# A graph layer on one core: one-hot columns by destination modulo 128, strip halves added on VectorE, means scaled on ScalarE, one-column counts, dense work in pieces

## The chip, the cores and the metric

The kernel runs on one core of one Trainium2 chip. The metric is the time of the whole program on the device in microseconds (us); lower is better. TensorE is called PE below, VectorE DVE, ScalarE ACT, GpSimd POOL and SyncE SP, as in the profile.

## The reference

For 12500 nodes with 256 features and 212500 edges (sorted by destination):

```
xn   = layernorm(x)
sum  = segment_sum(xn[src], dst);  cnt = segment_sum(1, dst)
agg  = sum / max(cnt, 1)
gnn  = relu(agg @ W_l.T + b_l + xn @ W_r.T) + xn
q, k, v = xn @ wq + bq, xn @ wk + bk, xn @ wv + bv        # 8 heads of 32
q, k = elu(q) + 1, elu(k) + 1
mix  = (q (k^T v)) / (q sum(k) + 1e-6) @ wo + bo
x1   = x + gnn + mix
out  = x1 + mixture_of_experts(layernorm(x1))             # the 2 best of 8 experts, then a layernorm
```

## The kernel before

Stage 1 normalises all rows and writes them to a table in HBM, each row as two float16 halves of 256 (a high and a low part, scaled by XS = 2048), and builds the matrices of the linear attention (`M_s`, `KS_s`). Stage 3, the subject here, goes over NB = 49 blocks of BN = 256 nodes. Stage 5 is the two-expert layer.

A block of stage 3 has TB = 34 edge tiles of 128 edges (the last block 29, so 1661 in all). For each tile POOL issues one indirect DMA (L643) that gathers 128 rows of the table, by the indices in `idxb`, into `msgs` (in the buffer `ring`). DVE makes the tile's one-hot matrix in float16 by comparing `iota_f` with the destinations in `edges` (`one_hots`, L1334; output `oh`, in the buffer `ohh`), and PE multiplies it with the gathered rows (L1076, into `pa`) and adds up the counts as a row (L1093, into `pc`: 128 columns, or two times 64).

Tiles come in 8 batches a block (`BATCH`). POOL waits for `idx_ready` and for `batch_used` of the same batch one block back; PE waits at each batch for `oh_ready` and for `gathered0` to `gathered7`; DVE waits in `one_hots` for `batch_used` half a block back. Each tile covers a window of 128 nodes that starts at `LO[k]`, a multiple of STRIP = 64. The sums of the tiles of one window are taken by DVE from PSUM (`take_strip`, L1354) as a strip, which overlaps its neighbours by half. When the block is over, PE joins its five strips by matmuls with an identity (`join_strips`, L1042), which also turns them, features to the partitions. The count row goes through ACT (`count_row`, L805) and a matmul with ones (`spread_counts`, L1003) to all partitions, where DVE makes a reciprocal of 256 (L1345) and scales the sums (`neighbours`, L1348).

The dense work of a block lies between its tiles, in each engine's own written order: `products` (L1015, 12 matmuls in float32), `turn_xn` (L981), `queries` (L990), `normalizers` (L997) and `turn_y` (L1027) on PE; `middle` (L1361 to L1369), `residual` (L1381, L1383), `middle_stats` (L1184 to L1214), `query_features` (L1388) and `normalise_queries` (L1394 to L1398) on DVE. The work of block b on block b - 1 starts at tile 6, `products` at tile 11, `normalizers` at tile 22.

## Time and profile before

| what | value |
|---|---|
| time, median of 3 runs (lowest, highest) | 3031.16 us (3028.17, 3031.72) |
| time of the profiled execution | 3025.19 us |
| its span, first to last instruction | 3023.7 us |
| first and last gather start | 264.2 us, 2376.4 us |
| PE, DVE, ACT, POOL busy over the span | 82%, 57%, 26%, 66% |

The table's shares are averages over three stages. Stage 3 is the stretch between the first and the last gather and a few microseconds after, some 70% of the span. POOL's busy time there is the gathers alone; the time between two of them is not counted as busy.

### The profile page before, as it was taken

What the parts mean: (1) busy time and instruction counts of PE and PEld (TensorE: products, weight loads), DVE (VectorE), ACT (ScalarE), POOL (GpSimd) and SP (SyncE); (2) the same over time, 40 slices, a digit from 0 to 9 for tenths busy, and PEclk for the clock granted to TensorE, in tenths of its full rate; (3) what the DMA queues carried; (4) which work ended last, traced back from release to release, by engine and by line L of the source; (5) the groups of instructions that cost most, each with busy time, mean ns of one, the idle gap of its engine ahead of it and who ended that gap; (6) DMA issues with size and microseconds to landing.
All of it is one profiled execution on the core that took longest, in us unless ns stands there. A gap on an engine that the chain in (4) does not pass through costs nothing.

```text
span 3023.7 us, 38535 instructions
## 1 busy us (share of the span) xinstructions
PE 2475.3 (82%) x11532; PEld 1605.7 (53%) x11532; DVE 1724.4 (57%) x3502; ACT 774.0 (26%) x1810; POOL 1991.1 (66%) x1831
## 2 busy tenths in 40 slices
PE   6888778787887788778877887788778699999997
PEld 5665434443444344434444444444444388888886
DVE  7885455445545554555455545554555566666666
ACT  4553011111111111111111111111111155555554
POOL 5446777777777777777777777777777334444443
PEclk9998777877787777777877787877777799999999
DMA  5333344434444444444444444444444322111221
GB/s 143 107 101 97 115 125 123 120 116 123 125 118 118 124 124 116 122 124 125 116 121 124 124 118 120 124 126 116 121 123 125 94 70 62 62 62 62 66 75 49
DMA packets 192238, 327.01 MB, mean 108 GB/s; under 512 B 32703, under 2 KB 138216, under 8 KB 192200
## 3 DMA queue, kind: packets, MB, share of 16 engines
q0 software_dynamic: 80160, 219.14, 25.4%
q1 hardware_dynamic: 111624, 107.01, 11.3%
q10 hardware_dynamic: 416, 0.39, 0.1%
q8 instruction: 19, 0.31, 0.0%
q14 instruction: 19, 0.16, 0.0%
HBM read 275.21 MB, written 51.20 MB: 108 GB/s over the span
## 4 chain that ended last, share of the span: by engine, by line
POOL 28%; PE 26%; issue 20%; DVE 15%; DMA 7%; ACT 2%; POOLq 0%; DVEq 0%; ACTq 0%; SPq 0%
POOL ring L643 20%; PE pd L1015 8%; PE pa L1076 6%; PE pd L1042 6%; DMA ring<-xn_table,idxb 4%; PE pc L1093 2%; POOL work L672 2%; POOL work L657 2%; POOL work L655 2%; DVE bst L1184 2%; PE pc L1003 2%; DMA work<-x_rows 2%; DVE nh L1211 1%; DMA out<-work 1%; DVE nv L1206 1%
## 5 line engine op out<-in xcount | busy, mean ns | idle before, releaser
L643 POOL DMA_INDIRECT ring<-xn_table,idxb x1661 | 1607.5, 968 | 509.7 <-issue 489.9
L1076 PE MATMUL pa<-ring,ohh 128*128 128x512 f16 x1661 | 767.7, 462 | 222.5 <-DMA ring<-xn_table,idxb 206.5
L1354 DVE TENSOR_REDUCE ring<-pa 128x256 f32<-128x512 f32 x196 | 135.4, 691 | 586.1 <-PE pa L1076 585.5
L1093 PEld LDWEIGHTS pc<-ohh,ones_h 128*1 128x1 f16 x2045 | 133.7, 80 | 535.7 <-issue 535.7
L1093 PE MATMUL pc<-ohh,ones_h 128*1 128x128 f16 (+1 forms) x2045 | 384.7, 219 | 0.0
L1076 PEld LDWEIGHTS pa<-ring,ohh 128*128 128x128 f16 x1661 | 173.1, 104 | 350.1 <-issue 172.1
L1136 PE MATMUL pd<-parts 128*128 128x256 f32 (+1 forms) x1568 | 314.6, 284 | 33.8 <-DVE parts L1524 33.8
L1136 PEld LDWEIGHTS pd<-parts 128*128 128x128 f32 (+1 forms) x1568 | 253.4, 188 | 51.4 <-DVE parts L1524 44.4
L1334 DVE TENSOR_TENSOR ohh<-iota_f,edges 128x512 f16<-128x512 f32 (+1 forms) x391 | 272.8, 718 | 0.9 <-issue 0.9
L997 PE MATMUL pd<-work,KS_s 128*128 128x256 f32 x196 | 100.7, 669 | 198.6 <-DVE work L1388 198.6
L769 ACT ACTIVATE work<-pd 128x512 f32<-128x512 f32 (+1 forms) x49 | 29.2, 596 | 881.5 <-PE pd L981 881.5
L1042 PEld LDWEIGHTS pd<-ident,ring 128*128 128x128 f32 x976 | 204.8, 321 | 31.6 <-issue 31.3
L1136 PE MATMUL pd<-W_lo_t,parts 128*128 128x256 f32 x784 | 220.1, 281 | 0.0
L1042 PE MATMUL pd<-ident,ring 128*128 128x128 f32 (+1 forms) x976 | 213.4, 413 | 0.0
L655 POOL TENSOR_TENSOR work<-work,ohh 128x1024 f32<-128x1024 f32 (+1 forms) x25 | 62.8, 2511 | 212.9 <-DMA work<-x_rows 163.5
L1015 PE MATMUL pd<-mats,work 128*128 128x256 f32 x784 | 193.1, 390 | 0.0
L1524 DVE TENSOR_TENSOR parts<-ring,parts 128x512 fp32r<-128x512 f32 (+1 forms) x100 | 121.9, 1219 | 109.6 <-ACT parts L855 109.6
L997 PEld LDWEIGHTS pd<-work,KS_s 128*128 128x128 f32 x196 | 57.1, 322 | 214.0 <-DVE work L1388 205.4
L1396 DVE RECIPROCAL work<-work 128x512 f32<-128x512 f32 x49 | 164.3, 3353 | 1.7
L1015 PEld LDWEIGHTS pd<-mats,work 128*128 128x128 f32 x784 | 147.0, 193 | 21.9
L1136 PEld LDWEIGHTS pd<-W_lo_t,parts 128*128 128x128 f32 x784 | 147.3, 188 | 7.9
L1524 DVE TENSOR_TENSOR parts<-M_s,parts 128x512 fp32r<-128x512 f32 (+1 forms) x100 | 100.1, 1001 | 71.7 <-ACT parts L855 71.5
(188 smaller groups left out, 3684.0 us busy)
## 6 DMA issues: line engine op xcount, KB each, us to landing
ring<-xn_table,idxb POOLq DMA_INDIRECT x1661, 2.7
yT<-in_x SPq DMA_DIRECT2D x24, 512.0 KB, 4.0
xn_table<-ring SPq DMA_DIRECT2D x24, 512.0 KB, 4.8
work<-in_x SPq DMA_DIRECT2D x48, 256.0 KB
x_rows<-work SPq DMA_DIRECT2D x48, 256.0 KB
y_rows<-work SPq DMA_DIRECT2D x48, 256.0 KB
work<-y_rows SPq DMA_DIRECT2D x24, 512.0 KB, 4.3
work<-x_rows SPq DMA_DIRECT2D x24, 512.0 KB, 4.0
```

Source lines behind the costliest of these rows:

```text
L643: pool.indirect_dma_start(out=msgs[:, k, :, :].rearrange("p s d -> p (s d)"), out_offset=None, in_=xn_table[:, :], in_offset=bass.Indirect ...
L655: pool.tensor_tensor(y_in[u][:, 0:n, :], y_in[u][:, 0:n, :], b2m[:, :].unsqueeze(1).to_broadcast([P, n, D]), ALU.add).then_inc(s["yb_made" ...
L997: ins = mm(pd[:, 0, c * BN:(c + 1) * BN], KS_s[:, c, :], pq[:, c * BN:(c + 1) * BN], start=True, stop=True)
L1015: ins = mm(pd[:, 2 + h, at:at + D], a[:, c * BN + h * P:c * BN + (h + 1) * P], w[:, c, :], start=a is xT2 and c == 0, stop=a is not xT2 an ...
L1042: ins = mm(pd[:, 0, c * BN + c0:c * BN + c1], strips[:, (NS * u + t + 1) % KEPT, c * P:(c + 1) * P], ident[:, c0 - STRIP * t:c1 - STRIP * ...
L1076: ins = mm(pa[:, t % 2, :], oh[:, slot, :], msgs[:, k, :, :].rearrange("p s d -> p (s d)"), start=begins, stop=ends, skip_group_check=True)
L1093: ins = mm(pc[0:1, v, c0:c1], ones_h[:, 0:1], oh[:, slot, o0:o1], start=first, stop=closing, skip_group_check=True)
L1136: ins = mm(pd[0:n, 2 * u + t // 2, (t % 2) * D:(t % 2 + 1) * D], hp[:, t * P:t * P + n], wp[:, f, :], start=f == 0 and t % 2 == 0 and hp i ...
L1334: V.tensor_tensor(oh[:, slot:slot + m, :], bc(iota_f[:, :], m), where, ALU.is_equal)\
L1354: V.tensor_reduce(strips[:, (NS * u + t + 1) % KEPT, :], pa[:, t % 2, :].rearrange("p (s d) -> p d s", s=PARTS), AX.X, ALU.add)\
L1396: V.reciprocal(qb, qb).then_inc(s["nrm_rec"], 1)
L1524: V.tensor_tensor(h_lo[f % HS][:, 0:w], h_full[f % 2][:, 0:w], h_hi[f % HS][:, 0:w], ALU.subtract)\
```

## The change

The window of a tile is no longer counted from `LO[k]`: the column of a destination is the destination modulo 128 (`iota_f` has 64 more columns, and `one_hots` reads it from `LO % 128`). So the two halves of a block's own strips sit on the partitions where the neighbouring strips have theirs. DVE adds the halves (`join_strips`, now on DVE: one instruction on 64 partitions for both groups, two on the other 64), each a sum of two operands in SBUF. The counts are a column beside each strip's sums: PE makes it with the one-hot as weights and one column of ones, DVE copies it from PSUM in `take_strip`, adds it with the halves and takes the reciprocal of 128x2. ACT scales the strips (`scale_sums`), PE turns them by 4 transposes (`turn_sums`), and DVE copies them from PSUM (`take_sums`). `count_row` and `spread_counts` are gone. PE's dense work is cut into pieces of one half each that go ahead of single tiles (`DENSE`), and batches now end where windows end.

```diff
-    BATCH = [(0, 4), (4, 8), (8, 12), (12, 17), (17, 21), (21, 25), (25, 29), (29, 34)]
+    BATCH = [(0, 4), (4, 8), (8, 13), (13, 17), (17, 21), (21, 25), (25, 30), (30, 34)]
...
-        strips = ring[:, MSGS:MSGS + KEPT * D].rearrange("p (n d) -> p n d", d=D)
+        strips = ring[:, MSGS:MSGS + KEPT * SW].rearrange("p (n d) -> p n d", d=SW)
...
+            def scale_sums(d, u):
+                act.wait_ge(s["cnt_rec"], d + 1)
+                for g in range(2):
+                    own = strips[:, NS * u + 2 * g + 1, 0:D]
+                    ins = nc.scalar.activation(own, own, ACT.Copy, scale=cnts[:, g:g + 1])
+                ins.then_inc(s["strips_scaled"], 1)
...
-            def count_row(d, v):
-                act.wait_ge(s["agg_done"], d + 1)
-                wait(act, s["agg_taken"], d)
-                nc.scalar.activation(rc[0:1, :], pc[0:1, v, 0:BN], ACT.Copy).then_inc(s["cnt_row"], 1)
...
+                    if not is_int(b, 0):
+                        scale_sums(b - 1, 1 - u)
...
+            def product(a, w, at, d, h):
                 for c in range(C):
+                    ins = mm(pd[:, 2 + h, at:at + D], a[:, c * BN + h * P:c * BN + (h + 1) * P], w[:, c, :],
+                             start=a is xT2 and c == 0, stop=a is not xT2 and c == C - 1, skip_group_check=True)
+                return ins
...
+            def neighbour_product(d, h):
+                pe.wait_ge(s["agg_taken"], d + 1)
+                ins = product(aggS, wlT, 0, d, h)
+                if h == 1:
+                    ins.then_inc(s["o_made"], 1)
...
-            def join_strips(d, u):
-                sums = strip_sums(d)
-                pe.wait_ge(s["strip_taken"], NS * d + len(sums))
+            def turn_sums(d, u):
+                pe.wait_ge(s["strips_scaled"], d + 1)
                 wait(pe, s["nrm_eps"], d + 1)
-                for t in sums:
-                    c0, c1 = max(STRIP * t, 0), min(STRIP * t + P, BN)
+                for g in range(2):
                     for c in range(C):
-                        ins = mm(pd[:, 0, c * BN + c0:c * BN + c1], strips[:, (NS * u + t + 1) % KEPT, c * P:(c + 1) * P],
-                                 ident[:, c0 - STRIP * t:c1 - STRIP * t], start=t == -1 and c == 0, stop=t == sums[-1],
-                                 skip_group_check=True)
+                        ins = nc.tensor.transpose(pd[:, 0, c * BN + g * P:c * BN + (g + 1) * P],
+                                                  strips[:, NS * u + 2 * g + 1, c * P:(c + 1) * P], ident[:, :])
                 ins.then_inc(s["agg_made"], 1)
-            JOIN = 6
-            HOOKS = ((11, products, 1), (11, turn_xn, 0), (13, queries, 0), (22, normalizers, 0), (26, turn_y, 1))
+            DENSE = {1: (root_product, 0, 1), 2: (root_product, 1, 1), 3: (mixed_product, 0, 1),
+                     4: (mixed_product, 1, 1), 12: (neighbour_product, 0, 1), 13: (neighbour_product, 1, 1),
+                     16: (queries, 0, 0), 17: (queries, 1, 0), 24: (normalizers, 0, 0), 25: (normalizers, 1, 0)}
+            TURN_SUMS, TURN_X, TURN_Y = 9, 14, 27
...
-                        if k == JOIN and not is_int(b, 0):
-                            spread_counts(b - 1, 1 - u)
-                            join_strips(b - 1, 1 - u)
-                        for at_tile, work, back in HOOKS:
-                            if k == at_tile and not (back and is_int(b, 0)):
-                                work(b - back)
+                        dense(b, k, u)
...
-                        ins = mm(pa[:, t % 2, :], oh[:, slot, :], msgs[:, k, :, :].rearrange("p s d -> p (s d)"),
-                                 start=begins, stop=ends, skip_group_check=True)
-                        if ends:
-                            ins.then_inc(s["strip_done"], 1)
-                        parts = []
-                        for db in (-1, 0, 1):
-                            c0, c1 = max(LO[k], db * BN), min(LO[k] + WIN, (db + 1) * BN)
-                            if c0 < c1 and not (db < 0 and is_int(b, 0)) and not (db > 0 and last_block):
-                                parts.append((db, c0 - db * BN, c1 - db * BN, c0 - LO[k]))
-                        for db, c0, c1, o0 in parts:
-                            v = (u + db) % 2
-                            first = (db == 1 and LO[k - 1] + WIN <= BN) or (is_int(b, 0) and k == 0)
-                            if db == 1 and first:
-                                wait(pe, s["agg_taken"], b)
-                            closing = (db == -1 and LO[k + 1] >= 0) or (last_block and k == LAST - 1)
-                            o1 = o0 + c1 - c0
-                            ins = mm(pc[0:1, v, c0:c1], ones_h[:, 0:1], oh[:, slot, o0:o1], start=first, stop=closing,
-                                     skip_group_check=True)
-                            if closing:
-                                ins.then_inc(s["agg_done"], 1)
-                    if ks and not (last_block and ks[-1] == LAST - 1):
+                        mm(pa[:, t % 2, :], oh[:, slot, :], msgs[:, k, :, :].rearrange("p s d -> p (s d)"),
+                           start=begins, stop=ends, skip_group_check=True)
+                        ins = mm(pc[:, t % 2, 0:1], oh[:, slot, :], ones_h[:, 0:1], start=begins, stop=ends,
+                                 skip_group_check=True)
+                    if ks:
                         ins.then_inc(s["batch_used"], 1)
...
-                V.tensor_tensor(oh[:, slot:slot + m, :], bc(iota_f[:, :], m), where, ALU.is_equal)\
+                c0 = LO[ks[0]] % WIN
+                V.tensor_tensor(oh[:, slot:slot + m, :], bc(iota_f[:, c0:c0 + WIN], m), where, ALU.is_equal)\
                     .then_inc(s["oh_ready"], 1)
-            def neighbours(d, u):
-                dve.wait_ge(s["cnt_spread"], d + 1)
+            def join_strips(d, u):
+                low, high = slice(0, STRIP), slice(STRIP, P)
+                own = strips[:, NS * u + 1:NS * u + 4:2, :]
+                last = is_int(d, NB - 1)
+                dve.wait_ge(s["strip_taken"], NS * d + (NS if last else NS + 1))
+                V.tensor_tensor(own[low, :, 0:D + 1], own[low, :, 0:D + 1], strips[low, NS * u:NS * u + 3:2, 0:D + 1], ALU.add)\
+                    .then_inc(s["halves_added"], 1)
+                for g in range(1 if last else 2):
+                    V.tensor_tensor(own[high, g, 0:D + 1], own[high, g, 0:D + 1],
+                                    strips[high, (NS * u + 2 * g + 2) % KEPT, 0:D + 1], ALU.add)\
+                        .then_inc(s["halves_added"], 1)
+                dve.wait_ge(s["halves_added"], 3 * d + (2 if last else 3))
+                V.tensor_scalar(cnts[:, :], own[:, :, D], 1.0, XS, ALU.max, ALU.mult).then_inc(s["cnt_max"], 1)
+                dve.wait_ge(s["cnt_max"], d + 1)
+                V.reciprocal(cnts[:, :], cnts[:, :]).then_inc(s["cnt_rec"], 1)
+                dve.wait_ge(s["cnt_rec"], d + 1)
+            def take_sums(d):
                 wait(dve, s["o_made"], d)
                 wait(dve, s["x1_made"], d)
-                wait(dve, s["agg_taken"], d)
-                V.tensor_scalar(rc[:, :], pc[:, u, BN:2 * BN], 1.0, XS, ALU.max, ALU.mult).then_inc(s["cnt_max"], 1)
-                dve.wait_ge(s["cnt_max"], d + 1)
-                V.reciprocal(rc[:, :], rc[:, :]).then_inc(s["cnt_rec"], 1)
-                dve.wait_ge(s["cnt_rec"], d + 1)
                 dve.wait_ge(s["agg_made"], d + 1)
-                V.tensor_tensor(pair(aggS), pair(pd[:, 0, :]), bc(rc[:, :], 2), ALU.mult)\
-                    .then_inc(s["agg_taken"], 1)
+                V.tensor_copy(aggS, pd[:, 0, :]).then_inc(s["agg_taken"], 1)
             def take_strip(b, t, u):
-                dve.wait_ge(s["strip_done"], NS * b + t + 2)
-                V.tensor_reduce(strips[:, (NS * u + t + 1) % KEPT, :], pa[:, t % 2, :].rearrange("p (s d) -> p d s", s=PARTS),
-                                AX.X, ALU.add)\
-                    .then_inc(s["strip_taken"], 1)
+                dve.wait_ge(s["batch_used"], NBT * b + 2 * t + 3)
+                kept = strips[:, (NS * u + t + 1) % KEPT, :]
+                V.tensor_reduce(kept[:, 0:D], pa[:, t % 2, :].rearrange("p (s d) -> p d s", s=PARTS), AX.X, ALU.add)
+                V.tensor_copy(kept[:, D:D + 1], pc[:, t % 2, 0:1]).then_inc(s["strip_taken"], 1)
...
-                    neighbours(d, 1 - u)
+                    join_strips(d, 1 - u)
+                    take_sums(d)
                     middle(d)
                     middle_stats(d)
                     return
                 for q in range(3):
                     one_hots(b, q)
                 take_strip(b, -1, u)
+                if not is_int(b, 0):
+                    join_strips(d, 1 - u)
                 one_hots(b, 3)
                 if not is_int(b, 0):
-                    neighbours(d, 1 - u)
+                    take_sums(d)
```

On DVE, at the start of the work of block b on block b - 1: before, after the strip of the tiles that end the old block (`ring<-pa`, with `ring` holding the strips). `rc` holds the counts and `work` the block's operands.

```order
L1354 TENSOR_REDUCE ring<-pa 128x256 [waits strip_done]
L1334 TENSOR_TENSOR ohh<-iota_f,edges 128x640 [waits batch_used]
L1343 TENSOR_SCALAR rc<-pc 128x256 [waits x1_made,agg_taken,o_made,cnt_spread]
L1345 RECIPROCAL rc<-rc 128x256 [waits cnt_max]
L1348 TENSOR_TENSOR work<-pd,rc 128x512 [waits agg_made,cnt_rec]
L1334 TENSOR_TENSOR ohh<-iota_f,edges 128x512 [waits batch_used]
```

The same place in the changed kernel, with its own line numbers:

```order
L1366 TENSOR_REDUCE ring<-pa 128x256 [waits batch_used]
L1367 COPY ring<-pc 128x1
L1343 TENSOR_TENSOR ring<-ring 64x2x257 [waits strip_taken]
L1346 TENSOR_TENSOR ring<-ring 64x257 x2
L1350 TENSOR_SCALAR cnts<-ring 128x2 [waits halves_added]
L1352 RECIPROCAL cnts<-cnts 128x2 [waits cnt_max]
L1334 TENSOR_TENSOR ohh<-iota_f,edges 128x512 [waits batch_used,cnt_rec]
L1360 COPY work<-pd 128x512 [waits agg_made,x1_made,o_made]
```

Three additions with both inputs in `ring` have come in, and the reciprocal is over 2 columns in place of 256; the 512-element operation on `pd` is a copy.

On PE, before, from the second batch of a block on (`gathered1`): the join stands in one piece between the tiles.

```order
L1076 MATMUL pa<-ring,ohh 128x512 [waits strip_taken,gathered1,oh_ready]
L1093 MATMUL pc<-ohh,ones_h 1x128
L1076 MATMUL pa<-ring,ohh 128x512
L1093 MATMUL pc<-ohh,ones_h 1x128
L1003 MATMUL pc<-rc,ones 128x256 [waits cnt_row]
L1042 MATMUL pd<-ident,ring 128x64 [waits nrm_eps,strip_taken]
L1042 MATMUL pd<-ident,ring 128x64
L1042 MATMUL pd<-ident,ring 128x128 x6
L1042 MATMUL pd<-ident,ring 128x64 x2
```

The changed kernel, from its third batch on:

```order
L1091 MATMUL pa<-ring,ohh 128x512 [waits gathered2,oh_ready]
L1093 MATMUL pc<-ones_h,ohh 128x1
L1045 MATMUL pd<-ident,ring 128x128 [waits nrm_eps,strips_scaled]
L1045 MATMUL pd<-ident,ring 128x128 x3
L1091 MATMUL pa<-ring,ohh 128x512
L1093 MATMUL pc<-ones_h,ohh 128x1
L1091 MATMUL pa<-ring,ohh 128x512
L1093 MATMUL pc<-ones_h,ohh 128x1
L1091 MATMUL pa<-ring,ohh 128x512
L1093 MATMUL pc<-ones_h,ohh 128x1
L1009 MATMUL pd<-mats,work 128x256 [waits agg_taken]
L1009 MATMUL pd<-mats,work 128x256
```

Ten matmuls and the spreading of the counts have become four transposes that stand three tiles later, and the product with the neighbours' means follows in two pieces at tiles 12 and 13 instead of behind the other products at tile 11.

## Rows read from the trace of the kernel before

**Rows 1.** The page: span, busy line, granted clock in 40 slices.

```profile
span 3023.7 us, 38535 instructions
...
PE 2475.3 (82%) x11532; PEld 1605.7 (53%) x11532; DVE 1724.4 (57%) x3502; ACT 774.0 (26%) x1810; POOL 1991.1 (66%) x1831
...
PEclk9998777877787777777877787877777799999999
```

**Rows 2.** Line L643 (the gathers): ns min/median/max, starts, idle before them.

```profile
L643 POOL DMA_INDIRECT ring<-xn_table,idxb x1661: 942/946/1599, 264.2 to 2376.4; - x185
...
  issue: 489.9, 1596
  ACT idxb L732: 10.1, 33
  PE pc L1093: 9.8, 32
...
DMA to landing us min/median/max: 2.6/2.7/4.3
```

**Rows 3.** Timeline, three stretches: start us, us, engine, line, [idle before].

```profile
382.38 1.27 POOL L643 DMA_INDIRECT ring<-xn_table,idxb  x1 [0.30 <-issue]
...
728.67 0.95 POOL L643 DMA_INDIRECT ring<-xn_table,idxb  x1 [0.30 <-issue]
729.13 0.69 DVE L1381 TENSOR_TENSOR work<-work 128x512 f32<-128x512 f32 x1
729.85 0.69 DVE L1383 TENSOR_TENSOR work<-work,bo_b 128x512 f32<-128x512 f32 x1
729.92 1.44 POOL L643 DMA_INDIRECT ring<-xn_table,idxb  x1 [0.30 <-issue]
...
2372.43 1.17 POOL L643 DMA_INDIRECT ring<-xn_table,idxb  x1 [0.30 <-issue]
```

**Rows 4.** Timeline, around DVE's reciprocal of 512.

```profile
1431.45 3.35 DVE L1396 RECIPROCAL work<-work 128x512 f32<-128x512 f32 x1
...
1432.18 0.95 POOL L643 DMA_INDIRECT ring<-xn_table,idxb  x1 [0.30 <-issue]
```

**Rows 5.** Groups in 1200 to 1800 us: count, busy us, mean ns, idle before.

```profile
L1334 DVE TENSOR_TENSOR ohh<-iota_f,edges 128x512 f16<-128x512 f32 x84 | 55.2, 685 | 0.0
...
L790 ACT ACTIVATE work<-work,nmr,rstd 128x256 f32<-128x256 f32 x28 | 15.3, 592 | 71.4 <-DVE nmr L1214 71.4
...
L1210 DVE TENSOR_TENSOR nh<-ny 128x2 f32<-128x2 f32 x42 | 6.8, 162 | 1.5
```

**Rows 6.** Groups in 268 to 280 us, on DVE.

```profile
L1316 DVE COPY yT<-pd 128x512 f32<-128x512 f32 x1 | 0.7, 693 | 0.4 <-PE pd L957 0.4
...
L1319 DVE TENSOR_TENSOR yT<-pd,yT 128x256 f32<-128x256 f32 x1 | 0.4, 424 | 2.9 <-PE pd L964 2.9
```

**Rows 7.** Groups in 1200 to 1800 us (14 blocks), on PE.

```profile
L1076 PE MATMUL pa<-ring,ohh 128*128 128x512 f16 x475 | 218.7, 460 | 60.3 <-DMA ring<-xn_table,idxb 60.1 <-issue 0.2
L1093 PE MATMUL pc<-ohh,ones_h 128*1 128x128 f16 (+1 forms) x586 | 109.7, 219 | 0.0
...
L1042 PE MATMUL pd<-ident,ring 128*128 128x128 f32 (+1 forms) x280 | 62.0, 417 | 0.0
```

**Rows 8.** Windows: busy of PE, PEld, DVE, ACT, POOL, clock, DMA share, GB/s.

```profile
1400.00:1800.00 400.00, 321.18 (x1311) 176.87 (x1311) 205.93 (x375) 56.74 (x201) 304.12 (x315) 0.77 0.42 121
1405.00:1408.00 3.00, 3.00 (x16) 3.00 (x16) 1.82 (x2) 0.00 (x0) 2.39 (x3) 0.50 0.41 126
```

**Rows 9.** The chain that ended last, 2384 to 2394 us: start us, us, what.

```profile
2384.98 0.38 ACT rc L805
...
2386.10 1.98 PE pd L1042 x16
2388.08 5.20 PE pd L1015 x24
2393.30 0.70 DVE work L1361
```

81 lines of the change are left out of this document (44 added, 37 removed).

## The prediction

> **What bounds the kernel now.** I read the page first, for which engine is full [rows 1]: PE looks fullest, 82% of the span, but its granted clock swings between the two levels in the middle stage, and POOL, at 66%, has nothing in the other stages that would show it as the bound. So I went to the gathers by themselves [rows 2]. From the first start at 264.2 us to the last at 2376.4 us lie 2112.2 us and 1660 steps, 1.272 us each. The median gather takes 0.946 us. The idle time before all 1661 is 489.9 + 10.1 + 9.8 = 509.8 us, 0.307 us each; the single rows show 0.30 [rows 3], also where a semaphore is named as the releaser. That gap is POOL's own step from one gather to the next, not a wait: no buffer, no index and no PE work has held a gather back. 0.946 + 0.303 is 1.249 us, and 1660 of those are 2073 us. What is left, about 39 us, is gathers that took longer than the median: mean 968 ns (1607.5 us of busy time over 1661) less 946 ns, times 1661, is 36.5 us, and a few us more lie in front of the first ones. Stage 3 is therefore 2073 us of gathers back to back, plus 36 us of stretched gathers, plus a tail behind the last gather.
>
> What stretches a gather is seen in the timeline [rows 3]. The gather at 728.67 runs its 0.95 us. The next starts at 729.92, 0.07 us after DVE began L1383, an addition with both inputs in SBUF; it takes 1.44 us, 0.49 longer, and the addition ends at 730.54, 0.62 us into the gather. DVE's long reciprocal with a single input runs over a whole gather and leaves it at 0.95 us [rows 4]. I set all 1661 gather rows beside DVE's rows. 129 gathers took over 1.0 us, and in 128 of them a DVE instruction with two SBUF inputs was running 0.1 us after the gather's start; the gather then lasts until that instruction ends and some 0.82 us more. An instruction that begins later, or has ended by then, costs nothing. Summed by DVE line: one_hots (L1334, 391 instructions) 24.3 us over 83 gathers; L1383 (49) 6.2 us over 14, the first and last of them at 382.38 and 2372.43 [rows 3]; L1381 (49) 4.1 us over 19; L1364 (49) 0.8; L1388 (49) 0.3; L1398 (49) nothing. So it is the phase of an instruction against the gathers that decides, and lines differ from 0 to 0.13 us per instruction.
>
> **The change part by part.** PE: the join's 280 matmuls in 14 blocks took 62.0 us [rows 7], 4.4 us a block; four transposes at its mean of 0.22 us are 0.9, so 3.5 us less. The count matmuls took 109.7 us in 14 blocks, 7.8 a block; 34 one-column ones cost at least nothing and at most the 0.10 us that I allow for a second pass of the weights, some 3.4, so at least 4.4 us less. The spreading of the counts goes too. PE gets about 8 us of 43.3 us a block back (34 x 1.272). None of it reaches the end: PE waits 60.3 us for gathers in those 14 blocks already [rows 7], and gathers do not wait for PE. It grows PE's waits for landings, no more. Nor does a gather start to wait for `idxb`: ACT issues the indices of the next block's first batches ahead of its new scaling, and the others are wanted a third of a block or more later.
>
> DVE: out go the reciprocal over 256, the scaling from PSUM and a short operation on PSUM, all with at most one SBUF input; by rows 4 they held up no gather, so removing them gives nothing. In come per block a copy from PSUM of 512 (0.69, [rows 6], one input: nothing), 4 copies of one column (0.16, after the smallest instruction [rows 5]: nothing, from PSUM), two tiny steps, and the join: one addition of 64 x 2 x 257 elements, in length like 128x512 (0.69, as one_hots, [rows 5]), and two of 64x257 (0.42 each, as 128x256, [rows 6]). All three have both inputs in SBUF. No row shows them. From below: nothing, as L1398 in all its 49. From above: every block stretches one gather by the longest seen, 1.599 - 0.946 = 0.65 us, and a second by a short one, 0.3: 0.95 x 48 = 46 us. I take the rate of the two additions in the middle of a block that are triggered as this one is, by work of PE whose clock varies: (4.1 + 6.2) / 98 = 0.105 us per 0.69 us instruction. What an instruction costs goes with the square of its length (the chance to be hit, times what remains), so a 0.42 us one costs 0.37 of that: 0.105 x 1.74 = 0.18 us a block, **+9 us** over 48 blocks.
>
> The Trainium skill, page "SBUF — State Buffer", section "Who interferes with whom", has two things on this. An instruction of DVE with two SBUF inputs contends with a GpSimd instruction that reads SBUF, and the loser waits for the whole instruction; with evenly spread phases that makes (0.69^2 + 2 x 0.42^2) / 2 / 1.25 = 0.33 us a block, 16 us, nearly twice what I take. The same section infers that tensor_tensor does not hold up descriptor generation; by that the join costs nothing. The stretched gathers [rows 3] are on the side of the first; the second is a rival below.
>
> The tail: after the last tile ACT's count row starts at 2384.98 and `middle` at 2393.30 [rows 9], 8.3 us. Now: strip 0.69 and column 0.16, additions 0.69 + 0.42, two tiny steps 0.4, scaling 2 x 0.59 [rows 5], four transposes 0.9, copy 0.69, and the last third of the products 5.20 / 3 = 1.7 [rows 9]: 6.8, and some 0.5 for the handovers, 7.3: 1 us less. The last tile itself can end earlier. Its gather starts at 2376.4 and lands 2.7 us later [rows 2], so four tiles at 0.7 us (L1076 0.46 and L1093 0.22, [rows 7]) could be done by 2382; now it is 2385, since PE is behind. With join and spreading off PE this comes 1 to 3 us sooner, less if `normalise_queries` (0.69 + 3.35 + 0.69) is then what DVE still has in front of the last strip. Together **-3.5 us** (-1 to -5).
>
> Stages 1 and 5 are not touched. The existing stretches, 36 us, are drawn anew: each batch now ends, and each one-hot starts, at another phase. I put no shift on them in the sum and +-15 us in the range.
>
> Sum against the profiled execution: 3025.2 + 9 - 3.5 = 3030.7 us. That execution is 6.0 us under the median of the runs, so from the median: 3031.2 + 5.5 = **3036.5 us**. A measurement of this kernel can tell about 0.2%, 6 us, from no change.
>
> **The rivals.**
> A. The forecast: the gathers stay the bound, the join costs about 9 us, old stretches stay within 7 us. 3036.5, own range 3029 to 3044. Chance 0.38.
> B. The one-hots fall into a bad phase. PE now often starts a batch right at its landing, so each `batch_used` and the one-hots behind it recur at one phase in every block. For: many of the 391 one-hots do sit in tight phases today, and cost 0.06 us each, half of L1381 and L1383's 0.105. If they go to that, 391 x 0.043 = +17 us on top: 3031.2 + 5.5 + 17 = 3054. Against: the phase could as well be good. It decides from where a one-hot still runs 0.1 us into a gather. Chance 0.24, clearly slower.
> C. The phases turn out better: one-hots and middle fall by half, -18 us, join +5: 3031 - 3.5 + 5 - 18 = 3015. For: L1398 and L1388 show lines with next to none. Chance 0.24, faster.
> D. The new additions cost nothing, the rest stays: 3031.2 - 3.5 = 3027.7, no change. Against: the stretched gathers [rows 3]. Chance 0.10.
> E. PE becomes the bound. Its granted clock is 0.50 (1.2 GHz) in one stretch, and 0.77 on the mean of 400 us, a mixture with the full 2.4 GHz [rows 8], where it is busy 0.80 x 43.3 = 34.7 us a block. Less 8 is 26.7, and all at 0.5 that is 26.7 x 0.77 / 0.5 = 41 us, plus the stalls behind DVE's query features. That touches 43.3; 1 us over it in 48 blocks is 3079. It decides when the clock never rises and DVE's results come late. For: more idle PE brings more low clock. Against: POOL has a block of slack. Chance 0.04. The Trainium skill, page "TensorE: Matmul & The Clock Gate", section "HAM oscillation", says that matmul bursts with waits between them fall back to the half clock each time; by that PE would sit low most of a block, which rows 8 show for part of it.
>
> **The numbers.** C ends below 3015 in some cases, B and E above 3054: range 3010 to 3060. Slower by over 0.2% (above 3037.2): B, E and two fifths of A, which straddles that bound, 0.24 + 0.04 + 0.15 = 0.43. Within: the rest of A and D, 0.23 + 0.10 = 0.33. Faster: C, 0.24.
>
> **What would show it.** Right: gathers still 0.30 us apart without a wait; busy time of the gather line near 1616 us (1607.5 + 9), the new stretches with the 64-partition additions running at their start; PE's waits for gathers above 60.3 us per 14 blocks; `middle` of the last block starting 12 to 16 us after the last gather's start in place of 16.9. Wrong: gaps above 0.30 before gathers (E, or indices late), a busy time of the gather line outside 1595 to 1630 (B, C), or the additions running over a gather's start without stretching it (D).

## The result, and the profile after

The changed kernel takes 3046.94 us (median of 6, 3041.0 to 3051.26), the kernel before in the same comparison 3029.54 us: a ratio of 1.0056, interval 1.0040 to 1.0072. It is slower by 17 us. Times and ratios here are of executions in the chip's faster state; one execution, of the additions alone below, fell in the slower one (3168.65 us, clock 0.683) and is left out. The profiled execution has a span of 3042.1 us, against 3023.7 before [rows 1].

The page of the kernel after, its span, busy line and granted clock:

```profile
span 3042.1 us, 36310 instructions
...
PE 2121.0 (70%) x10270; PEld 1450.6 (48%) x10270; DVE 1726.7 (57%) x3845; ACT 800.2 (26%) x1859; POOL 2009.3 (66%) x1831
...
PEclk9998767776776677767767777777667699999999
...
POOL 52%; issue 25%; DVE 9%; DMA 6%; PE 5%; ACT 2%; POOLq 1%; DVEq 0%; ACTq 0%; SPq 0%
```

PE went from 82% to 70% of the span, and the kernel became slower all the same: the engine that the change relieves is not the one that sets the end. The last line is the chain that ended last: POOL and its issue steps are 77% of it.

Groups by line of the kernel after (count, busy us, mean ns, idle before and its releasers), answering to [rows 2, 5, 6, 7], and the window that answers to [rows 8]:

```profile
L645 POOL DMA_INDIRECT ring<-xn_table,idxb x1661 | 1625.0, 978 | 509.8 <-issue 498.0 <-ACT idxb L734 10.4 <-PE pc L1093 1.5
L1091 PE MATMUL pa<-ring,ohh 128*128 128x512 f16 x1661 | 710.6, 496 | 780.2 <-DMA ring<-xn_table,idxb 645.0 <-DVE ohh L1334 122.5 <-issue 11.7
L1093 PE MATMUL pc<-ones_h,ohh 128*128 128x1 f16 x1661 | 314.7, 189 | 0.0
L1366 DVE TENSOR_REDUCE ring<-pa 128x256 f32<-128x512 f32 x196 | 135.4, 691 | 658.5 <-PE pc L1093 658.0
```
```profile
1400.00:1800.00 400.00, 251.14 (x1053) 143.72 (x1054) 202.46 (x434) 61.26 (x207) 305.23 (x312) 0.70 0.42 120
```

Idle time before the gathers is 509.8 us, as before; no gather waits for more than its 0.30. Their busy time grew by 17.5 us (1607.5 to 1625.0), and the last gather starts 17.5 us later (2393.9 against 2376.4). PE's busy time in the window fell from 321.18 to 251.14 us, 7.6 us a block of 43.3, and all of that went into waits: for landings it waits 645.0 us now, 206.5 before. A new wait for the one-hots, 122.5 us against 3.9, lies there too. The granted clock fell from 0.77 to 0.70, without touching the end. So this is a loss on POOL, whose code the change leaves alone.

Where it sits, from the timeline of the kernel after. First `normalise_queries` of one block (reciprocal L1407, product L1409), then the join of a later one:

```profile
1219.94 3.35 DVE L1407 RECIPROCAL work<-work 128x512 f32<-128x512 f32 x1
...
1222.57 0.94 POOL L645 DMA_INDIRECT ring<-xn_table,idxb  x1 [0.30 <-issue]
1223.33 0.69 DVE L1409 TENSOR_TENSOR work<-work 128x512 f32<-128x512 f32 x1
1223.82 1.01 POOL L645 DMA_INDIRECT ring<-xn_table,idxb  x1 [0.30 <-issue]
...
1411.95 0.69 DVE L1366 TENSOR_REDUCE ring<-pa 128x256 f32<-128x512 f32 x1 [11.08 <-PE pc L1093]
1411.99 0.95 POOL L645 DMA_INDIRECT ring<-xn_table,idxb  x1 [0.30 <-issue]
...
1412.74 0.69 DVE L1343 TENSOR_TENSOR ring<-ring 64x514 f32<-64x514 f32 x1
1413.24 1.00 POOL L645 DMA_INDIRECT ring<-xn_table,idxb  x1 [0.31 <-issue]
1413.45 0.76 DVE L1346 TENSOR_TENSOR ring<-ring 64x257 f32<-64x257 f32 x2
...
1414.55 0.94 POOL L645 DMA_INDIRECT ring<-xn_table,idxb  x1 [0.30 <-issue]
```

The reciprocal, one input, is running when the gather at 1222.57 starts, and this gather keeps 0.94. L1409, two inputs in SBUF, still has 0.20 us to run when the gather at 1223.82 starts: 1.01. In the join the gather at 1411.99 runs beside the one-input L1366 and keeps 0.95; the one at 1413.24 starts inside L1343, two inputs in SBUF, which ends 0.19 us later: 1.00. The two L1346 start 0.21 us into this gather or later, end before the next, and cost nothing here. These two are small hits; the mean one at L1409 is 11.7 / 38 = 0.31 us.

I set all gather rows beside DVE's rows once more. For each gather of more than 1.00 us I took what it has over 0.95 us, and summed by the DVE line that runs 0.1 us after its start (by this measure the kernel before has 35.4 us over 129 gathers):

| line of DVE | before | after |
|---|---|---|
| one-hots, L1334 | 24.0 us, 83 gathers | 20.6 us, 92 |
| product with the reciprocal, L1398 / L1409 | 0 | 11.7, 38 |
| query features, L1388 / L1399 | 0.3, 1 | 5.9, 31 |
| bias added to the rest, L1383 / L1394 | 6.2, 14 | 6.0, 16 |
| sum of the rest, L1381 / L1392 | 4.0, 19 | 1.6, 7 |
| join, L1343 and L1346 | none | 3.1 + 2.6, 10 and 16 |
| all (with small ones) | 35.4, 129 | 52.3, 218 |

The join, 5.7 us, is a third of the 16.9 us. The rest comes from two old instructions whose length didn't change, only the time of their start: together they gained 17.3 us, and other lines lost some 6.

The end, from the chain that ended last in the kernel after (start us, us, what), answering to [rows 9]:

```profile
2393.93 3.55 DMA ring<-xn_table,idxb
2397.48 0.14 issue
2397.61 0.59 PE pa L1091
...
2400.05 0.45 PE pa L1091
2400.49 0.00 PE pc L1093
2400.50 4.92 PE pd L1009 x16
2405.42 0.45 PE pd L1045 x4
...
2405.99 0.70 DVE work L1360
2406.69 0.04 issue
2406.74 2.01 PE pd L1009 x8
2408.74 0.02 issue
2408.77 0.70 DVE work L1372
```

From the last gather's start to `middle` (L1372) are 14.84 us; it was 16.9. The last tile is done by 2400.50, and then the 8 matmuls of the root and mixing products (L1009, x16 in the row since each of these matmuls shows twice there, 4.92 us) stand on PE in front of the transposes (L1045).

### The profile page after: what moved, and what is told of

It reads as the page before. It is cut to its first block, busy times and chain, and to the rows that moved or that the text cites. A ratio compares the mean times of both kernels' runs of the same rounds, so it can differ in the third digit from the quotient of the medians.

```text
span 3042.1 us, 36310 instructions
## 1 busy us (share of the span) xinstructions
PE 2121.0 (70%) x10270; PEld 1450.6 (48%) x10270; DVE 1726.7 (57%) x3845; ACT 800.2 (26%) x1859; POOL 2009.3 (66%) x1831
## 3 DMA queue, kind: packets, MB, share of 16 engines
q0 software_dynamic: 80160, 219.14, 25.5%
q1 hardware_dynamic: 111624, 107.01, 11.1%
## 4 chain that ended last, share of the span: by engine, by line
POOL 52%; issue 25%; DVE 9%; DMA 6%; PE 5%; ACT 2%; POOLq 1%; DVEq 0%; ACTq 0%; SPq 0%
POOL ring L645 44%; DMA ring<-xn_table,idxb 2%; POOL work L674 2%; POOL work L659 2%; POOL work L657 2%; PE pa L1091 2%; DMA work<-x_rows 2%; DVE bst L1182 1%; DMA out<-work 1%; ACT yT L686 1%; DVE nv L1204 1%; PE pd L1009 1%; DVE yT L1220 1%; POOL mats L669 1%; DVE nh L1209 1%
## 5 line engine op out<-in xcount | busy, mean ns | idle before, releaser
L645 POOL DMA_INDIRECT ring<-xn_table,idxb x1661 | 1625.0, 978 | 509.8 <-issue 498.0
L1091 PE MATMUL pa<-ring,ohh 128*128 128x512 f16 x1661 | 710.6, 496 | 780.2 <-DMA ring<-xn_table,idxb 645.0
L1091 PEld LDWEIGHTS pa<-ring,ohh 128*128 128x128 f16 x1661 | 198.7, 120 | 1103.8 <-issue 670.3
L1366 DVE TENSOR_REDUCE ring<-pa 128x256 f32<-128x512 f32 x196 | 135.4, 691 | 658.5 <-PE pc L1093 658.0
L1009 PE MATMUL pd<-mats,work 128*128 128x256 f32 x784 | 331.3, 565 | 2.7 <-DVE work L1360 2.7
L1093 PE MATMUL pc<-ones_h,ohh 128*128 128x1 f16 x1661 | 314.7, 189 | 0.0
L1334 DVE TENSOR_TENSOR ohh<-iota_f,edges 128x512 f16<-128x512 f32 (+1 forms) x391 | 272.5, 718 | 7.6 <-issue 0.9
L1009 PEld LDWEIGHTS pd<-mats,work 128*128 128x128 f32 x784 | 204.8, 288 | 78.6 <-issue 31.7
L772 ACT ACTIVATE ring<-ring,cnts 128x256 f32<-128x256 f32 x98 | 44.5, 501 | 741.5 <-DVE cnts L1352 741.5
L1093 PEld LDWEIGHTS pc<-ones_h,ohh 128*128 128x128 f16 x1661 | 179.4, 108 | 70.5 <-issue 42.1
L1407 DVE RECIPROCAL work<-work 128x512 f32<-128x512 f32 x49 | 164.3, 3353 | 1.7
L807 ACT ACTIVATE yT<-pd 128x256 f32 (+2 forms) x98 | 36.7, 380 | 454.6 <-PE pd L1034 454.6
L1405 DVE TENSOR_SCALAR work<-pd 128x512 f32<-128x512 f32 x49 | 33.9, 692 | 184.0 <-PE pd L1002 184.0
L1119 PE MATMUL pa<-parts 128*128 128x512 f32 (+1 forms) x400 | 124.3, 393 | 6.6 <-DVE W_lo_t L1510 6.6
```

What stands on the lines that cost most here:

```text
L645: pool.indirect_dma_start(out=msgs[:, k, :, :].rearrange("p s d -> p (s d)"), out_offset=None, in_=xn_table[:, :], in_offset=bass.Indirect ...
L1009: ins = mm(pd[:, 2 + h, at:at + D], a[:, c * BN + h * P:c * BN + (h + 1) * P], w[:, c, :], start=a is xT2 and c == 0, stop=a is not xT2 an ...
L1091: mm(pa[:, t % 2, :], oh[:, slot, :], msgs[:, k, :, :].rearrange("p s d -> p (s d)"), start=begins, stop=ends, skip_group_check=True)
L1093: ins = mm(pc[:, t % 2, 0:1], oh[:, slot, :], ones_h[:, 0:1], start=begins, stop=ends, skip_group_check=True)
L1119: ins = mm(hbank(f)[:, 0:w], wp[:, e, c, fc * P:(fc + 1) * P], yp[u][:, c, 0:w], start=c == 0 and wp is W1_hi and yp is y_hi, stop=c == C ...
L1334: V.tensor_tensor(oh[:, slot:slot + m, :], bc(iota_f[:, c0:c0 + WIN], m), where, ALU.is_equal)\
```

## The experiments

The first four ran on one chip, where the kernel before takes 3029.79 us.

**The join with one input.** Each of the three additions becomes a sum over an axis of one element, as long, but reading one place; the neighbours' halves are left out of the means.

```
-  V.tensor_tensor(own[low, :, 0:D + 1], own[low, :, 0:D + 1], strips[low, NS * u:NS * u + 3:2, 0:D + 1], ALU.add)
+  V.tensor_reduce(own[low, :, 0:D + 1], own[low, :, 0:D + 1].unsqueeze(3), AX.X, ALU.add)
...
```

> The changed kernel, in which the three additions of the join are tensor_reduce over an axis of one element: same sizes and place, but a single SBUF input. It leaves out the neighbouring halves, so its sums and counts lack them. Lock theory (a gather waits while a DVE instruction with two SBUF inputs runs at its start): no gather over 1.0 us with a join instruction at its start, where the changed kernel has 26 such gathers and 5.7 us; gather line busy about 1619 us against 1625.0; time about 6 us under the changed kernel's 3047, so some 3041. Rival (the stretches come from the traffic of DVE on SBUF or from the place of the join, whatever its inputs): stretches at the join stay, 3047.

Measured: 3037.4 us, ratio 1.0023 (1.0013 to 1.0033). The instructions take the same time (0.68 and twice 0.37), over gathers that stay at 0.95:

```profile
1018.08 0.68 DVE L1343 TENSOR_REDUCE ring<-ring 64x514 f32<-64x514 f32 x1
1018.79 0.75 DVE L1346 TENSOR_REDUCE ring<-ring 64x257 f32<-64x257 f32 x2
1018.83 0.95 POOL L645 DMA_INDIRECT ring<-xn_table,idxb  x1 [0.31 <-issue]
...
1028.80 0.68 DVE L1334 TENSOR_TENSOR ohh<-iota_f,edges 128x512 f16<-128x512 f32 x1
1028.85 1.45 POOL L645 DMA_INDIRECT ring<-xn_table,idxb  x1 [0.30 <-issue]
```

The first gather shown starts 0.04 us after a one-input instruction began and is not touched; the second starts 0.05 us after a two-input one began and takes 0.50 us longer. In the whole run 53 gathers have a join instruction running 0.1 us after their start, and none is stretched; in the changed kernel it is 51, and 26 of them are. So the stretch is gone though the meetings are as many. The gather line is 4.6 us shorter (1620.4), and the time fell as expected. L1408 (the product) keeps 7.8 us, L1398 (the features) 5.4.

**The reciprocal in PSUM.** `normalise_queries` leaves sum and reciprocal in their PSUM bank, so that the product has one input in SBUF.

```
...
-  V.reciprocal(qb, qb).then_inc(s["nrm_rec"], 1)
+  V.reciprocal(pd[:, 0, :], pd[:, 0, :]).then_inc(s["nrm_rec"], 1)
...
-  V.tensor_tensor(pq, pq, qb, ALU.mult).then_inc(s["qhat_made"], 1)
+  V.tensor_tensor(pq, pq, pd[:, 0, :], ALU.mult).then_inc(s["qhat_made"], 1)
```

> The changed kernel with the reciprocal of the normaliser left in PSUM, so that the product of queries and reciprocal (512 elements) has one SBUF input; PE's next use of that bank waits for the product. Lock theory: the 38 gathers and 11.7 us that this product stretches in the changed kernel go to 0; gather line busy about 1613, time about 3035, if the other phases stay. Rival (phases only trade: the stretch goes to another instruction of the same block): 0 at the product, but one-hots or the strip's followers rise by as much, 3047.

Measured: 3037.5 us, 1.0019 (1.0011 to 1.0028), span of the profiled run 3038.7. The product runs 0.1 us after the start of 36 gathers and stretches none (before the edit 44, of which 38 were stretched, by 11.7 us), but the one-hots have 28.2 us in place of 20.6, and the gather line is at 1621.9: of 11.7 us taken away 3.1 are left in the profiled execution. The time came near the expected 3035 us, the gather line did not come to the expected 1613: here the rival, that the stretch goes elsewhere in the block, holds for the larger part.

**The additions alone.** The kernel before with three additions of the join's sizes in a spare piece of `ring`, at the place where the changed kernel has its join: behind the first strip of a block and ahead of its fourth one-hots. Nobody reads their result.

```
+  V.tensor_tensor(spare[0:STRIP, 0:514], spare[0:STRIP, 1028:1542], spare[0:STRIP, 514:1028], ALU.add)
+  for g in range(2):
+      V.tensor_tensor(spare[STRIP:P, 257 * g:257 * (g + 1)], spare[STRIP:P, 1028:1285], spare[STRIP:P, 514:771], ALU.add)
...
```

> The kernel before with three more additions on DVE, of 64x514, 64x257 and 64x257 elements, both inputs in a spare part of the ring buffer, at the place where the changed kernel has its join; nobody reads their result. Lock theory: a few us in stretches at these additions, 3 to 16 (5.7 in the changed kernel, 9 forecast), plus up to 10 us either way where the 1.5 us shift the instructions behind them to other phases: 3030 to 3052. Rival (the added work costs nothing because POOL does not wait for DVE): 3030, gather line busy 1607.

Measured: 3037.2 us (median of six), 1.0028 (1.0014 to 1.0042). The additions stretch 35 gathers by 4.7 + 3.5 = 8.2 us, and the gather line grows by 9.3 (1616.8), inside what was expected. The product with the reciprocal still stretches nothing.

**The table of batches alone.** The kernel before with the changed `BATCH` and nothing else: the same instructions, the same sizes.

```
-  BATCH = [(0, 4), (4, 8), (8, 12), (12, 17), (17, 21), (21, 25), (25, 29), (29, 34)]
+  BATCH = [(0, 4), (4, 8), (8, 13), (13, 17), (17, 21), (21, 25), (25, 30), (30, 34)]
```

> The kernel before with the batch limits of the changed kernel and nothing else: the five-tile batches are the third and the seventh in place of the fourth and the eighth. No instruction is added, only one-hots and waits lie one tile earlier or later. Phase theory: the gather line's busy time moves by 5 to 15 us in either direction from 1607.5, and the time with it. Rival (the loss belongs to the added instructions): 3030, busy time within 2 us of 1607.5.

Measured: 3032.96 us, 1.0015 (1.0006 to 1.0024). The gather line grows by 6.5 us (1614.0). The query features, L1388, stretch 41 of 49 gathers by 5.8 us, where they had 1 and 0.3 us, as L1399 does in the changed kernel (31, 5.9). The product stays nearly harmless (8 gathers, 0.7 us), so the table explains the features, not the product. The line's growth is inside the expected 5 to 15 us.

The group of the gather line in these kernels, in the order table alone, additions alone, join with one input, reciprocal in PSUM (before: 1607.5 us busy [rows 2]):

```profile
L643 POOL DMA_INDIRECT ring<-xn_table,idxb x1661 | 1614.0, 972 | 509.8 <-issue 492.7 <-ACT idxb L732 11.9 <-PE pc L1093 5.2
```
```profile
L643 POOL DMA_INDIRECT ring<-xn_table,idxb x1661 | 1616.8, 973 | 509.9 <-issue 494.1 <-ACT idxb L732 8.2 <-PE pc L1093 7.6
```
```profile
L645 POOL DMA_INDIRECT ring<-xn_table,idxb x1661 | 1620.4, 976 | 509.9 <-issue 493.5 <-ACT idxb L734 15.2 <-PE pc L1093 1.2
```
```profile
L645 POOL DMA_INDIRECT ring<-xn_table,idxb x1661 | 1621.9, 976 | 509.7 <-issue 490.6 <-ACT idxb L734 17.1 <-PE pc L1093 2.1
```

The idle time is 509.7 to 509.9 us in all six kernels, so the busy time of this line is all that moves. Span less last gather's start is 645.3 to 648.2 us in the six (before 647.3, after 648.2): the end follows the last gather, by a constant. TensorE's mean granted clock doesn't order the times: the additions alone, at 0.834, take as long as the reciprocal in PSUM, at 0.789.

**Eight runs on a second chip.** These ran, in two sets of four, on another chip, where the kernel before takes 3861.91 and 3858.6 us, and in every kernel the gathers are held up. The edits are, on the changed kernel: TensorE adds the high and low halves of a row itself, by two matmuls of 256 columns into the same columns of PSUM (merged, and again merged_b, whose expectation below describes this edit wrongly: no even and odd edges are told apart); that, and the counting constant of the one-hots in a PSUM bank (merged_iota, merged_iota_b), the shortest of the edits to show:

```
-  V.tensor_tensor(oh[:, slot:slot + m, :], bc(iota_f[:, c0:c0 + WIN], m), where, ALU.is_equal)
+  V.tensor_tensor(oh[:, slot:slot + m, :], bc(pc[:, 0, c0:c0 + WIN], m), where, ALU.is_equal)
...
```

that, and the other long pairs of SBUF inputs fed from PSUM (all_psum); that, and the strips' halves added from PSUM as a strip is taken, so that the join's additions are gone, with a second copy of the normalised rows on ScalarE (fused); and, by itself on the changed kernel, the normaliser's pieces two tiles earlier (norm22, norm22_b):

```
-  16: (queries, 0, 0), 17: (queries, 1, 0), 24: (normalizers, 0, 0), 25: (normalizers, 1, 0)}
+  16: (queries, 0, 0), 17: (queries, 1, 0), 22: (normalizers, 0, 0), 23: (normalizers, 1, 0)}
```

> The changed kernel with the high and low halves of a row added by PE: two matmuls of 256 columns into the same 256 columns of PSUM in place of one of 512, the count column beside them in the same bank. DVE then takes a strip with one copy of 257 elements (0.42 us) in place of a reduce of 512 and a column copy (0.69 + 0.15 us), and two PSUM banks are free. It is the base for the two kernels that follow. No instruction with two SBUF inputs is added or removed: lock theory says only that phases shift, gather line busy 1610 to 1640, time 3033 to 3060. Rival (PE's load matters): 1661 more matmuls with their weight loads bring PE nearer to the bound, gaps before gathers above 0.30 us, 3060 and more.

> The kernel above with the column numbers that the one-hots compare against held in one of the free PSUM banks: every one_hots instruction (391) then has one SBUF input, nothing else changes. Lock theory: no gather over 1.0 us with a one_hots at its start, where the changed kernel has 92 such gathers and 20.6 us; time about 20 us under the kernel above. Rival (DVE's writing of the one-hots, or plain load, stretches gathers): the same time as the kernel above.

> As the kernel above, and also with one input in PSUM: the addition of the output bias (bias held in PSUM), the product with the normaliser, the query features (ScalarE leaves its second result in PSUM) and the addition of the residual to the rectified product. Two SBUF inputs are left in one 512-element addition a block and in the join's three. Lock theory: stretches of 5 to 12 us in all against 49 in the changed kernel and 36 in the one before; gather line busy 1580 to 1590; time 3000 to 3010, faster than both. Rival (what is removed at one place returns at the rest): 3025 to 3050.

> The changed kernel with the two pieces of the normaliser product ahead of tiles 22 and 23 in place of 24 and 25, one batch earlier. The product with the reciprocal, which stretched no gather in the kernel before and 11.7 us of gathers in the changed one, starts about 4.1 us after that PE work. Phase theory: it starts at another phase, so its 11.7 us change (most likely fall, as most of the period is harmless), time 3035 to 3050. Rival (its stretches belong to the clock and the load, not to the phase): still some 12 us there, 3047.

> The changed kernel in which TensorE adds the even and odd edges' sums itself: two products of 128x64 a batch into one accumulator in place of one of 128x128, the count in the same bank, and one copy on VectorE in place of a sum over pairs and a copy. The one-hots' comparison and the join stay as they are. Lock theory (a VectorE instruction with two SBUF inputs that runs just after a gather's start makes that gather last): the number of such instructions is that of the changed kernel, so the stretch over 0.95 us per gather stays at 35 to 60 us, the last gather starts at 2380 to 2400, and the time is 3030 to 3055. Rival, TensorE bound: 565 more matmuls of 64 columns (about 496 batches in the stage) lengthen TensorE's line beyond POOL's: gaps between gathers above 0.32 us appear and the time goes above 3060.

> The kernel merged_b with the counting constant of the one-hots held in a PSUM bank, so that the comparison has one SBUF input and one PSUM input; nothing else differs. Lock theory: the one-hots' part of the stretch (20 to 28 us in the kernels so far) goes to below 1 us, of which some comes back at the other instructions as phases are redrawn (at most 8 us), so 15 to 25 us below merged_b: ratio about 0.997 to 1.001 of the kernel before. Rival, clock theory (the time follows TensorE's granted clock, and the stretches are only a sign of it): the time stays within 5 us of merged_b.

> The changed kernel with no VectorE instruction of two SBUF inputs left in the gathers' path but the small ones on query features' first sum and the messages' short ones: constants in PSUM banks, feature and normaliser products fed from PSUM, the strips' halves added straight from PSUM when a strip is taken, so that the three additions of the join are gone. It computes the same outputs. Lock theory: stretch over 0.95 us below 5 us in all, gather line busy 1572 to 1582 us, the last gather starts at 264 + 1660 x 1.249 = 2338 to 2345, and the end follows by the same 655 us or less: 2990 to 3005, a ratio of 0.987 to 0.992. Rival, another engine takes over as the bound (TensorE at its lower clock is at some 84% of the stage): gathers get gaps above 0.32 us and the time stays at 3015 or more. Rival, clock theory: no less than 3025.

> The changed kernel with the two pieces of the normaliser product ahead of tiles 22 and 23 in place of 24 and 25, so that the chain of reciprocal and product on VectorE starts earlier in a block. Lock theory: the product with the reciprocal (11.7 us of the stretch in the changed kernel, 38 of 49 gathers) meets other phases of a gather, so its part changes anywhere between 0 and 12 us and the others are redrawn by up to 10 either way: 3032 to 3055. Rival, the order of TensorE's pieces doesn't matter: the same time as the changed kernel within 3 us and the same stretch at the product.

| kernel | us | ratio to before there (interval) | stretch by the measure above, us |
|---|---|---|---|
| merged | 3603.72 | 0.9320 (0.9292 to 0.9347) | 34.6 |
| merged_iota | 3597.09 | 0.9296 (0.9267 to 0.9325) | 13.4 |
| all_psum | 3597.96 | 0.9298 (0.9268 to 0.9327) | 11.5 |
| norm22 | 3664.07 | 0.9476 (0.9446 to 0.9505) | 37.9 |
| merged_b | 3608.01 | 0.9361 (0.9329 to 0.9393) | 35.4 |
| merged_iota_b | 3594.64 | 0.9323 (0.9292 to 0.9354) | 13.5 |
| fused | 3639.85 | 0.9432 (0.9399 to 0.9466) | 0.3 |
| norm22_b | 3667.76 | 0.9523 (0.9490 to 0.9556) | 38.3 |

The times miss all the expectations, which were made for a POOL that never waits. The expected stretches came: below 5 us in fused, 5 to 12 in all_psum (11.5), 35 to 60 in merged_b (35.4, at its edge). The busy time of the gather line is 1584.9 us in all_psum, inside its 1580 to 1590, and 1605.4 in merged, under its 1610 to 1640. One block of merged_iota_b shows what holds its gathers, PE first, then DVE, ACT and POOL:

```profile
1054.31 0.17 PE L1094 MATMUL pa<-ones_h,ohh 128*128 128x1 f16 x1
...
1066.97 0.37 PE L1092 MATMUL pa<-ring,ohh 128*128 128x256 f16 x1 [1.94 <-issue]
1069.07 0.37 PE L1092 MATMUL pa<-ring,ohh 128*128 128x256 f16 x1 [1.73 <-issue]
...
1076.77 0.18 PE L1094 MATMUL pa<-ones_h,ohh 128*128 128x1 f16 x1 [1.03 <-issue]
1080.93 1.11 PE L1045 MATMUL pd<-ident,ring 128*128 128x128 f32 x4 [3.98 <-ACT ring L772]
```
```profile
1077.59 0.43 DVE L1368 COPY ring<-pa 128x257 f32<-128x257 f32 x1 [28.64 <-remote]
```
```profile
1079.97 0.91 ACT L772 ACTIVATE ring<-ring,cnts 128x256 f32<-128x256 f32 x2 [34.62 <-DVE cnts L1354]
```
```profile
1072.13 0.95 POOL L645 DMA_INDIRECT ring<-xn_table,idxb  x1 [0.31 <-issue]
1078.37 1.19 POOL L645 DMA_INDIRECT ring<-xn_table,idxb  x1 [5.29 <-remote]
```

The matmul at 1054.31 is the last of the block's first batch, and the copy L1368 waits for nothing but that batch's `batch_used`; it starts 23.1 us later. In the changed kernel on the first chip this takes 0.04 us; in these eight runs the median over the blocks is 23 or 24 us. The join on DVE, the scaling on ACT and the transposes L1045 on PE stand behind that copy, and POOL behind PE's batches: it stands still for 5.29 us here, and some 7 us more at a block's edge for indices; both recur in most blocks. The gathers' data is not what is late. By the records of its packets, the last data packet of a gather ends 1.45 us (median) after the gather's instruction in all eight runs, and 1.46 or 1.47 us in the six on the first chip; and the gaps of 1 to 2 us on PE stand also between two matmuls of one tile, where PE waits for no gather. Whether the matmuls ran later than their records say, or the signal of the finished batch came late, the trace doesn't tell: it has 335 to 381 of the 391 signals of `batch_used` there. POOL's idle time is 1067 to 1145 us in these kernels, not 510. With such waits in the chain, 20 us less of stretch gives little: merged_iota_b is 13.4 us under merged_b, merged_iota 6.6 under merged, with intervals that overlap.

The stretches themselves are as readable there, and they are the test. Line L645, ns min/median/max and starts, of merged_b, then merged_iota_b, then fused:

```profile
L645 POOL DMA_INDIRECT ring<-xn_table,idxb x1661: 940/946/1467, 264.5 to 2932.6; - x185
```
```profile
L645 POOL DMA_INDIRECT ring<-xn_table,idxb x1661: 940/946/1437, 264.1 to 2925.8; - x185
```
```profile
L645 POOL DMA_INDIRECT ring<-xn_table,idxb x1661: 940/946/1083, 265.6 to 2975.3; - x185
```

With its constant in PSUM the comparison goes from 103 gathers and 23.7 us (merged_b; 100 and 22.5 us in merged) to none, in both pairs, though in merged_iota_b it still runs 0.1 us after the start of 108 gathers. In fused, where no long DVE instruction of stage 3 has two inputs in SBUF, 2 gathers of 1661 are over 1.0 us (1.08 the longest), and the line's busy time is 1570.2 us, 1661 times 0.945. That is the expected 1572 to 1582, and a little less. Whether fused gains on the first chip (1625.0 - 1570.2 = 55 us less of POOL is what it offers) was not measured; on this one it is 45 us slower than merged_iota_b, for a reason that I didn't find (it has 98 more instructions on ScalarE and other handovers). In merged_b the join's first addition, 49 instructions, stretches 45 gathers by 11.1 us, in the changed kernel 10 by 3.1: the same instruction, at another phase.

The two norm22 runs give the product 3.6 and 3.7 us (13 and 14 gathers) against 11.7, but on a chip where every phase is another, so they don't tell what the moved pieces do. They say one more thing. This kernel is the changed one but for two numbers, and is 5% faster there than the kernel before. The changed kernel itself was not run there.

## Why the prediction was right, and where its terms were off

Forecast: 3036.5 us, +5.5, most likely slower by over 0.2%. Measured +17 us by the ratio, +18.4 by the spans, inside the range. The mechanism held: what bounds the kernel, what stretches a gather, and that PE's relief gives nothing. The size did not. The sum gave a third of what came, 3046.94 lies outside the 3029 to 3044 of case A, and the gather line came to 1625.0, not near 1616. What kept the forecast inside its range was the 15 us either way for the old stretches, and that these went up was luck: the prediction gave B and C, up and down, 0.24 each. The terms, by spans:

- **POOL bounds, and the gap is POOL's own**: shown. Idle 509.7 to 509.9 us in the six kernels on the first chip, and the end 645 to 648 us behind the last gather's start in all of them.
- **Two SBUF inputs running at a gather's start stretch it**: shown by three exchanges, each taking its line's stretch to nothing while the line still ran at 53, 36 and 108 gathers' starts: the join's one-input form, the product from PSUM, the one-hots' constant in PSUM. In the changed kernel 217 of the 218 stretched gathers end 0.81 to 0.83 us after such an instruction; the one left is the first gather of all. The Trainium skill's page "SBUF — State Buffer", section "Who interferes with whom", says the same: a VectorE instruction with at most one SBUF input, outside the modes that use both ports, does not contend with GpSimd. Its inference that tensor_tensor leaves descriptor generation alone does not hold for these gathers, which also read their indices from SBUF (`idxb`): 38 are stretched at the 49 instructions of L1409, none with one input in PSUM.
- **PE gets 8 us a block back, and none of it reaches the end**: 7.6, and PE's waits for landings rose from 206.5 to 645.0 us.
- **The join costs 9 us**: 5.7 in the changed kernel, 8.2 in the kernel before with the additions alone. The rate from L1381 and L1383 was the right size; rival D, that they cost nothing, is refuted.
- **Old stretches drawn anew, no shift, 15 either way**: this was the term that was mis-sized. The gather line grew by 17.5 us, so with the join's 5.7 it is +11.8, two thirds of the loss. It isn't rival B: the one-hots fell from 24.0 to 20.6 us. L1409 came to 11.7 and L1399 to 5.9, the two lines that the prediction had quoted as harmless (rival C used them as proof that phases can be good). The features' part is shown: the batch table alone brings 5.8 us. What moved the product is narrowed only: neither the table alone (0.7) nor additions of the join's length in the kernel before (0) do it, and 7.8 us stay without the join's second input. What is left is the cut-up dense work, the new counts, or several parts together; none of these was tried by itself on the first chip.
- **The tail, -3.5 us**: -2.1. What was off is the list of what stands between the last tile and `middle`: I counted the last third of the products (1.7 us, measured 2.01) and missed that the other two thirds, root and mixing, 4.92 us, are ahead of the transposes once no later tile is there to hide them.
- **The stages behind**: taken as 0; from `middle` to the end 633.3 us against 630.4, +2.9, unexplained. Of the two other kernels with the change, the one-input join has 630.2 and the reciprocal in PSUM 633.3, so it need not come from the change.

The sum is 5.7 + 11.8 - 2.1 + 2.9 = 18.3 us. Rival E did not come: at a granted clock of 0.70 PE still waits more than before. What stays open in size: executions of the changed kernel lie between 3041 and 3051 us (that phases are redrawn in each is likely, not shown), so single profiles resolve some 5 us; removing the join's or the product's stretch changed the median by 9.5 us and the gather line by only 4.6 and 3.1.

## What to carry over

When one engine issues work back to back and another's instructions can stretch each piece, price an edit by what it does to the phases, not by its own work: here a change that relieved an engine with time to spare moved two instructions of unchanged length onto the starts of gathers, and that cost twice what the new additions did. A term "the old collisions are redrawn" needs a mean that looks at lines standing at nothing, since these can only get worse. The cure that doesn't depend on the phase is structural: with one of VectorE's two inputs in PSUM no gather was stretched, in all five kernels that did it for a line; what it gives in time was measured on the first chip for the product alone, and some of it came back elsewhere. And measure on more than one chip: the same pair can stand at +0.6% on one and its near twin at -5% on another.

## What the runs showed of the hardware

- An indirect gather of 128 rows holds POOL for 0.946 to 0.949 us (medians), and 0.30 us pass to the next when nothing holds it up, in all kernels of this study and on both chips. A VectorE instruction with two SBUF inputs, tensor_tensor on 64 partitions too, that runs 0.1 us after the gather's start adds up to 0.65 us (1.599 - 0.946); with one input in PSUM it adds nothing.
- On the second chip the kernel before takes 27% longer (3861.91 against 3029.79 us), though the packets of the gathers' queue occupy the DMA engines no longer. Queue rows of the kernel after and of merged_iota_b:

```profile
q0 software_dynamic: 80160, 219.14, 25.5%
```
```profile
q0 software_dynamic: 80160, 219.14, 21.1%
```

25.5% of 3042.1 is 776 us, 21.1% of 3592.3 is 758 us, for the same packets and bytes, and the packets of a gather end as soon behind it (1.45 against 1.47 us). What comes late there is what waits for PE's finished batches, by 23 us a block. Its cause, and why the kernel before suffers most from it, was not found.
